# An attention and FFN kernel whose selected weights come from one-hot products instead of gathers

## Chip, cores and metric

One core of a Trainium2 chip. The metric is the device time of one execution in microseconds, lower is better. Engines are TensorE (PE; PEld its weight loads), VectorE (DVE), ScalarE (ACT), GpSimd (POOL), and SyncE (SP), which only issues transfers here.

## What is computed

x is 32 sequences of 32 positions and 512 features in float32. `itok_B_0_30` picks one 32 x 32 matrix out of 32 for each sequence, `itok_B_0_7` an expert; `perm` permutes the features.

```
w = cond_weights[itok_B_0_30]                 # (32, 32, 32), one matrix per sequence
c = einsum('bct,bcd->bdt', x, w)
q, k, v = c @ wq.T, c @ wk.T, c @ wv.T        # 32 heads of 16
q, k = rope(q), rope(k)
x1 = x + softmax(causal(q k^T / 4)) v @ wo.T
h = x1 @ W.T + 2 * sum_e gates[e] * (x1 @ A[e].T) @ B[e].T   # gates: top 2 of 8, softmax
out = x1 + unpermute(down(gelu(up(permute(h)))))
```

## The kernel before

All is written for the five engines by hand: each engine has its own list of instructions, and every wait is on a semaphore (`d_...` for transfers). The 1024 rows are 8 tiles of 128 rows, four sequences each, worked in G = 4 groups g of two tiles t; a group's data stand as features x 256 rows in four chunks of 128. Large products are made in three passes of float32r values (high by high, high by low, low by high: `mm3`, L593 to L595), so each weight has a high half, a copy on ScalarE (`w_his`, L974), and a low half, a subtraction, on VectorE (`w_los`, L1217) or for wo on GpSimd (`wo_los`, L505).

TensorE's order (L589 on) is cond (the selected matrices, spread into `wbd` blocks), q, k, v, scores, the products with the probabilities (`pv`), wo, then the router, the low rank and W products (w2) and the FFN. The stages of successive groups are interleaved: while group g has its `pv`, TensorE makes q, k and v of group g+1. PSUM has eight banks in three rings, A (2: cond, q, k, v), S (2: scores, pv, down) and F (4). Work takes the banks of a ring in turn, and a bank is given back when its reader is done. So the second half of k of group 1 takes the bank from which VectorE's rope(1,1) reads, v(1,0) that of rope(1,2), and v(1,1) that of rope(1,3).

rope(g,i), i = 0, 1 for q and 2, 3 for k, runs on two engines. VectorE shuffles the bank into `rot` (L1261) and multiplies by cos (L1263); GpSimd multiplies `rot` by sin (L474) and adds (L478). There is one `rot` from group 1 on, so VectorE's rope(1,i+1) waits until GpSimd has added rope(1,i) (`ve.wait_ge(roped, n - 1)`). For group 0, rope(0,3) is VectorE's alone (L1269, L1273). k is then spread into `kbd` blocks (`k_blocks`, L489 on GpSimd, L1283 on VectorE). The softmax is max and subtraction on VectorE (`max_shift`, L1295, L1297), exp on ScalarE (L1018), sum and reciprocal on VectorE (`sums`, L1303, L1305), the scaling on GpSimd (`norm`, L535), `turn` on VectorE (L1311), and `probs_block` on ScalarE (L974).

The beginning. GpSimd gathers the rows of cond_weights of group 0 (`cond_rows`, L450) with indices that VectorE makes from the ids, then the 32 whole matrices (`cond_seqs`, L457), which SP writes to a scratch `rows` and reads back for groups 1 to 3 as `wg`. SP holds wq's second half, wk and wv back behind those gathers. Four gathers of w2 and B rows by perm (`perm_rows`, L465) follow on GpSimd once wk has landed; TensorE turns them (`prep_w2`, L602, `prep_b`, L610). Three of the gathered quarters lie in `kbd[1]`, so the k blocks of tile 1 wait for the last `prep_w2`. TensorE runs idle products (L825) while it waits for loads.

GpSimd's list for group 0 is then three ropes, four k blocks, a clearing of pbd, norm(0,0), norm(0,1), wo's low halves, rope(1,0), norm(0,2), norm(0,3), rope(1,1) to rope(1,3) and four k blocks of group 1.

Of the kernel before, what the change touches and what calls it, by code (L numbers as in the profile page):

```python
# [42 lines left out]
MASKED = -1.0e30  # L43

# [36 lines left out]
def build(nc, x, xT, who, wcond, wq, wk, wv, wo, w2b, wr, wa, up, down, perm, consts, cols, rows, out):  # L81
    ctx = ExitStack()
    with ctx:
# [12 lines left out]
        cst = sb("cst", [P, CW])  # L96
# [5 lines left out]
        wg = sb("wg", [P, TILES, T])  # L102
# [16 lines left out]
        small = sb("small", [P, 348])  # L119
        idx = sb("idx", [P, TILES], U32)  # L120
        permc = sb("permc", [P, KC], I32)
# [4 lines left out]
        def rows_of(tile):  # L126
# [7 lines left out]
        kbd1 = kbd[:, 1, :, :, :].rearrange("p c b k -> p (c b k)")  # L134
        WB = D + P
        raw_w2b = [xt[:, 1, :, :].rearrange("p c n -> p (c n)")[:, 0:WB]] + [kbd1[:, WB * c:WB * c + WB]
                                                                            for c in range(KC - 1)]
        raw_a = rows_of(x2[:, 0:2, :].rearrange("p a n -> p (a n)"))
        seq_rows = kr[0:B, :, :].rearrange("p c n -> p (c n)")
# [46 lines left out]
        ids = sb("ids", [P, 3, TILES], I32)  # L186
# [4 lines left out]
        ident = con("ident")  # L191

# [9 lines left out]
        def A(g, k):  # L202
            return "A", 8 * g + k

        def S_at(g):
            return 8 * g - 2 if g else 0

        def S_scores(g, i):
            if g == G - 1:
                return ("A", 8 * G + i) if i < 2 else ("S", S_at(g) + i - 2)  # L210
            return "S", S_at(g) + i

        def PVi(g, t):
            if g == G - 1:
                return "A", 8 * G + 2 + t
            return "S", S_at(g) + 4 + (2 if g else 1) * t
# [12 lines left out]

        f_fill(("w2", 0), ("w2", 1), ("w2", 2), ("b", 0), ("w2", 3))  # L230
# [20 lines left out]
        def Wi(g, i):  # L251
            return ("A", 8 * G + 6) if (g, i) == (G - 1, 1) else Fi(g, "W", i)

        def WOi(g, i):
            return ("A", 8 * G + 4 + i) if g == G - 1 else Fi(g, "WO", i)

        def UNi(i):
            return Fi(G - 1, "UN", 1) if i else ("A", 8 * G + 8)

        def Y_chunk(c):  # L260
            return ("A", 8 * G + 7) if c == KC - 1 else S_down(G - 1, c // 2)
# [15 lines left out]
        def wait_kbd(eng, g, t, c):  # L277

            s = (kbd_v, kbd_p)[c % 2] if g else (kbd_p, kbd_v)[c // 2]
            eng.wait_ge(s, 4 * g + 2 * t + (c // 2 if g else c % 2) + 1)  # L280
# [6 lines left out]
        def half_of(part, r):  # L287

            return xc[:, part, :, :].rearrange("p c (t r n) -> p c t r n", t=GT, r=2)[:, :, :, r, :]

        def by_half(item):
            return bank(item)[:, :].rearrange("p (c t n) -> p c t n", c=KC, t=GT)
# [17 lines left out]
        W_AT = {"wq": 0, "wk": 2, "wv": 4, "wo": 6, "a": 8}  # L310
# [52 lines left out]
        kbd_v, kbd_p, scored = sem("kbd_v"), sem("kbd_p"), sem("scored")  # L363
# [18 lines left out]
        def _(sp):  # L382
# [1239 lines left out]
```

## Time and profile before

| | us |
|---|---|
| median of 3 runs | 217.81 (217.02 to 218.19) |
| the profiled execution | 216.94 |
| its span | 215.1 |
| TensorE busy | 201.6 (94%) |
| VectorE busy | 147.3 (68%) |
| GpSimd busy | 122.4 (57%) |
| ScalarE busy | 114.2 (53%) |

The span is from the first to the last recorded instruction of one execution; the time of an execution is measured around it and is 1.84 us longer here. A timeline row gives start, duration, engine, line, and in brackets how long the engine had been idle and who ended that. A product in float32 is recorded as two rows.

### The profile page before, as it was taken

What the parts mean: (1) busy time and instruction counts of PE and PEld (TensorE: products, weight loads), DVE (VectorE), ACT (ScalarE), POOL (GpSimd) and SP (SyncE); (2) the same over time, 40 slices, a digit from 0 to 9 for tenths busy, and PEclk for the clock granted to TensorE, in tenths of its full rate; (3) what the DMA queues carried; (4) which work ended last, traced back from release to release, by engine and by line L of the source; (5) the groups of instructions that cost most, each with busy time, mean ns of one, the idle gap of its engine ahead of it and who ended that gap; (6) DMA issues with size and microseconds to landing.
All of it is one profiled execution on the core that took longest, in us unless ns stands there. A gap on an engine that the chain in (4) does not pass through costs nothing.

```text
span 215.1 us, 5966 instructions
## 1 busy us (share of the span) xinstructions
PE 201.6 (94%) x2536; PEld 175.2 (81%) x2536; DVE 147.3 (68%) x283; ACT 114.2 (53%) x189; POOL 122.4 (57%) x96
## 2 busy tenths in 40 slices
PE   4999698699999999999999999999999999798993
PEld 4989675598878999988679899986788987688863
DVE  2368799899488978775646877836769886158223
ACT  2173173692271536439983337289865866533460
POOL 6628996959786201487985201978997344425000
PEclk9999999999999999999999999999999999999999
DMA  6699983300001050000026320000044300134002
GB/s 202 194 375 292 337 282 101 91 11 3 0 3 53 0 186 12 5 0 5 0 27 76 101 97 0 3 0 3 0 52 94 56 5 3 10 38 52 0 3 98
DMA packets 10858, 15.43 MB, mean 72 GB/s; under 512 B 2288, under 2 KB 6544, under 8 KB 10832
## 3 DMA queue, kind: packets, MB, share of 16 engines
q1 hardware_dynamic: 8384, 11.99, 16.8%
q0 software_dynamic: 2160, 3.05, 8.7%
q8 instruction: 20, 0.33, 0.6%
q10 hardware_dynamic: 288, 0.01, 0.1%
q14 instruction: 6, 0.05, 0.1%
HBM read 11.25 MB, written 3.80 MB: 70 GB/s over the span
## 4 chain that ended last, share of the span: by engine, by line
PE 86%; DVE 7%; issue 3%; ACT 2%; DMA 1%
PE ps_A L593 12%; PE ps_A L595 11%; PE ps_A L594 11%; PE ps_F L593 8%; PE ps_F L594 7%; PE ps_F L595 7%; PE ps_S L699 6%; PE ps_F L789 4%; PE ps_A L625 4%; PE ps_S L804 3%; PE ps_S L825 3%; PE ps_S L677 3%; PE ps_A L699 1%; PE ps_A L817 1%; DMA cst<-constants 1%
## 5 line engine op out<-in xcount | busy, mean ns | idle before, releaser
L974 ACT ACTIVATE pbd<-pr 32x512 f32<-32x512 f32 x56 | 35.3, 630 | 5.9 <-DVE pr L1311 5.2
L535 POOL TENSOR_TENSOR pr<-pr,small 128x512 f32<-128x512 f32 x16 | 17.6, 1111 | 35.5 <-DVE small L1305 35.4
L474 POOL TENSOR_TENSOR rot<-rot,cst 128x512 f32<-128x512 f32 x14 | 19.1, 1361 | 15.0 <-DVE rot L1261 14.8
L515 POOL DMA_INDIRECT out<-y,row_at x12 | 19.8, 1646 | 11.3 <-ACT y L974 8.8
L1062 ACT ACTIVATE act<-ps_F 128x512 f32<-128x512 f32 x32 | 16.5, 603 | 11.2 <-PE ps_F L789 11.2
L1283 DVE TENSOR_TENSOR kbd<-kr,cst 128x512 f32<-128x512 f32 x16 | 20.7, 1320 | 2.4 <-POOL kr L478 2.4
L489 POOL TENSOR_TENSOR kbd<-kr,cst 128x512 f32<-128x512 f32 x16 | 20.1, 1283 | 2.1 <-PE ps_F L602 2.0
L593 PE MATMUL ps_A<-xc,wqT 128*128 128x256 f32 x64 | 18.2, 285 | 1.7 <-DVE xc L1229 1.7
L1018 ACT ACTIVATE pr<-pr 128x512 f32<-128x512 f32 x16 | 10.0, 631 | 16.4 <-DVE pr L1297 16.2
L593 PE MATMUL ps_A<-xc,wkT 128*128 128x256 f32 x64 | 18.3, 286 | 0.0
L594 PE MATMUL ps_A<-xc,wkT 128*128 128x256 f32 x64 | 17.9, 279 | 0.0
L594 PE MATMUL ps_A<-xc,wqT 128*128 128x256 f32 x64 | 17.9, 279 | 0.0
L595 PE MATMUL ps_A<-xc,wqT 128*128 128x256 f32 x64 | 17.9, 279 | 0.0
L595 PE MATMUL ps_A<-xc,wkT 128*128 128x256 f32 x64 | 17.8, 279 | 0.0
L593 PE MATMUL ps_F<-x,w2T 128*128 128x256 f32 x56 | 16.1, 287 | 0.0
L595 PE MATMUL ps_F<-x,w2T 128*128 128x256 f32 x56 | 15.6, 279 | 0.0
L594 PE MATMUL ps_F<-x,w2T 128*128 128x256 f32 x56 | 15.6, 279 | 0.0
L593 PEld LDWEIGHTS ps_A<-xc,wqT 128*128 128x128 f32 x64 | 12.0, 188 | 2.1 <-issue 1.4
L593 PE MATMUL ps_F<-xc,woT 128*128 128x256 f32 x48 | 13.7, 286 | 0.0
L593 PE MATMUL ps_A<-wvT,xc 128*128 128x512 f32 x32 | 13.5, 420 | 0.0
L594 PE MATMUL ps_F<-xc,woT 128*128 128x256 f32 x48 | 13.4, 280 | 0.0
L595 PE MATMUL ps_F<-xc,woT 128*128 128x256 f32 x48 | 13.4, 279 | 0.0
(187 smaller groups left out, 614.7 us busy)
## 6 DMA issues: line engine op xcount, KB each, us to landing
xs<-in_x SPq DMA_DIRECT2D x4, 512.0 KB, 6.3
xt<-in_xT SPq DMA_DIRECT2D x4, 512.0 KB, 3.3
out<-xt SPq DMA_DIRECT2D x3, 512.0 KB, 3.0
pbd<-in_L_attn_wq SPq DMA_DIRECT2D x2, 512.0 KB, 4.4
act<-in_L_attn_wk SPq DMA_DIRECT2D x1, 1024.0 KB, 6.2
act<-in_L_attn_wv SPq DMA_DIRECT2D x1, 1024.0 KB, 8.6
act<-in_L_attn_wo SPq DMA_DIRECT2D x1, 1024.0 KB, 10.0
out<-xt SPq DMA_DIRECT2D x2, 256.0 KB, 2.2
```

Source lines behind the costliest of these rows:

```text
L474: pool.tensor_tensor(rv, rv, con("sin").unsqueeze(1).to_broadcast([P, 2 * N // T, T]), ALU.mult).then_inc(rot_sin, 1)
L489: pool.tensor_tensor(kbd[:, t, c, :, :].rearrange("p b (h s) -> p b h s", h=HG), kv.unsqueeze(2).to_broadcast([P, BT, HG, T]), con("head") ...
L515: pool.indirect_dma_start(out=out, out_offset=bass.IndirectOffsetOnAxis(ap=row_at[:, g, c:c + 1], axis=0), in_=y[:, c, :], in_offset=None, ...
L535: pool.tensor_tensor(pr[:, i, :, :], pr[:, i, :, :], mx[:, i, :].unsqueeze(2).to_broadcast([P, NH // 2, T]), ALU.mult).then_inc(normed, 1)
L593: pe.matmul(dst, hi_l, hi_r, start=start, stop=False, skip_group_check=skip)
L594: pe.matmul(dst, hi_l, lo_r, start=False, stop=False, skip_group_check=skip)
L595: return pe.matmul(dst, lo_l, hi_r, start=False, stop=stop, skip_group_check=skip)
L699: last = pe.matmul(bank(it)[32 * j:32 * j + 32, P * c:P * c + P], vz_of(g, t)[:, 4 * c + j, HD * e:HD * e + 2 * HD], pbd_of(g, t, c // 2)[ ...
L974: return sc.activation(dst, src, ACT.Copy)
L1018: sc.activation(pr[:, i, :, :], pr[:, i, :, :], ACT.Exp, scale=float(HD) ** -0.5).then_inc(exped, 1)
L1062: sc.activation(act[:, r, j, :, :], bank(it)[:, :].rearrange("p (h n) -> p h n", h=2), ACT.Gelu).then_inc(s_free(it), 1)
L1283: ve.tensor_tensor(kbd[:, t, c, :, :].rearrange("p b (h s) -> p b h s", h=HG), kv.unsqueeze(2).to_broadcast([P, BT, HG, T]), con("head").u ...
```

## The change

The constants bring cond_weights along, laid out so that its 32 matrices lie on partitions. VectorE compares the ids with the partition number (a one-hot), 16 small products (`select`) pick the matrices, four transposes on VectorE put them into `wsel` for all groups, and the `wbd` blocks are made from `wsel`. The three gathers of cond_weights, `rows` and `wg` are gone. x of group 0 is loaded from ScalarE's queue, wq in three pieces, and SP issues wq, wk, wv and x1 with no wait between. GpSimd's `perm_rows` waits for wk as before, and now directly follows two clearings. The gathered rows lie in both halves of `xt`, in `y` and in the third buffer of `vz`, which is therefore cleared after the last `prep_w2`.

cond of group 0 goes to four banks, two chunks each; the q products of group 0 (`first_q`) take both halves chunk by chunk; q and k of group 0 lie in ring F. TensorE makes both v before the first scores, turns w2's quarters 0 and 1 after them, quarter 2 and B after cond(1), and quarter 3 after q of group 1. ScalarE takes three of the k blocks of tile (0,1).

```diff
@@ SP
-            load_x(0)
-            sp.dma_start(raw["wq"][:, 0:2, :], wq_rows[:, 0:2, :]).then_inc(d_w["wq"], 16)
-            sp.wait_ge(d_wg[0], 16)
+            sp.dma_start(raw["wq"][:, 0:1, :], wq_rows[:, 0:1, :]).then_inc(d_w["wq"], 16)
+            sp.dma_start(raw["wq"][:, 1:2, :], wq_rows[:, 1:2, :]).then_inc(d_wq1, 16)
             sp.dma_start(raw["wq"][:, 2:4, :], wq_rows[:, 2:4, :]).then_inc(d_wq2, 16)
-            sp.wait_ge(d_wg[1], 16)
             load_w("wk")
             load_w("wv")
-            sp.wait_ge(d_seq, 16)
-            sp.dma_start(rows, seq_rows).then_inc(d_rows, 16)
             load_x(1)
-            sp.wait_ge(d_rows, 16)
-            sp.dma_start(wg[:, GT:TILES, :],
...
@@ GpSimd
-            pool.wait_ge(idx_ready, 1)
-            cond_rows(0)
-            cond_rows(1)
+            pool.memset(pbd[:, 1, 0:HC, :, :], 0.0).then_inc(pbd_zero, 1)
             pool.wait_ge(d_ids, 16)
-            cond_seqs()
-            pool.memset(pbd[:, 1, :, :, :], 0.0).then_inc(pbd_zero, 1)
-            pool.wait_ge(d_permc, 16)
             pool.wait_ge(d_w["wk"], 16)
             perm_rows()
             for i in range(3):
                 rope(0, i)
-            for t in range(GT):
-                for c in range(2):
-                    k_blocks(0, t, c)
-            wait_w(pool, "wq")
+            k_blocks(0, 0, 0)
+            k_blocks(0, 0, 1)
+            k_blocks(0, 1, 0)
+            wait_w(pool, "wq", KC)
             pool.memset(pbd[:, 0, :, :, :], 0.0).then_inc(pbd_zero, 1)
+            pool.memset(pbd[:, 1, HC:2 * HC, :, :], 0.0).then_inc(pbd_zero, 1)
             for g in range(G):
                 more = g + 1 < G
                 if more:
                     norm(g, 0)
                     norm(g, 1)
                 if g == 0:
+                    wait_full(pool, prep("w2", KC - 1))
+                    pool.memset(vz[:, 2, :, :], 0.0).then_inc(vz_zero, 1)
                     wo_los()
@@ TensorE
+            def select(r):
+
+                it = Fi("sel", r)
+                rows = slice(T * r, T * r + T)
+                for j in range(BT):
+                    at = slice(T * j, T * j + T)
+                    last = pe.matmul(bank(it)[at, 0:SC * T], onehot[rows, at], wst[rows, :],
+                                     start=True, stop=True, skip_group_check=True)
+                last.then_inc(s_full(it), 1)
...
             pe.wait_ge(d_cst, 16)
-            idle_products(16)
-            cond(0, 0)
-            cond(0, 1)
-            idle_products(6)
-            qk(0, "wq", Q, 0)
-            qk(0, "wq", Q, 1)
-            qk(0, "wk", K_, 0)
-            qk(0, "wk", K_, 1)
+            idle_products(2, rings["S"][0])
+            pe.wait_ge(onehot_ready, 1)
+            for r in range(BT):
+                select(r)
+            idle_products(4, rings["S"][0])
+            first_conds()
+            idle_products(2, rings["F"][3])
+            first_q()
+            qk(0, "wk", 0)
+            qk(0, "wk", 1)
+            v(0, 0)
+            v(0, 1)
+            scores(0, 0)
             pe.wait_ge(d_w["w2b"], 16 * KC)
-            for k in range(KC - 1):
-                prep_w2(k)
-            prep_b()
-            wait_w(pe, "wv")
-            v(0, 0)
-            scores(0, 0)
-            prep_w2(KC - 1)
-            v(0, 1)
+            prep_w2(0)
+            prep_w2(1)
             cond(1, 0)
             cond(1, 1)
+            prep_w2(2)
+            prep_b()
             scores(0, 1)
...
                 if g == 0:
+                    prep_w2(KC - 1)
                     pv(0, 0, 0)
@@ ScalarE
             v_out(0, 0)
-            turned_hi(prep("w2", KC - 1), WT["w2"][:, 0, KC - 1, :])
+            for c in range(1, KC):
+                k_blocks(c)
+            v_out(0, 1)
+            turned_hi(prep("w2", 0), WT["w2"][:, 0, 0, :])
             exp(0, 0)
@@ VectorE
+            def turn_selected(r):
+
+                it = Fi("sel", r)
+                wait_full(ve, it)
+                ve.transpose(wsel[:, SC * r:SC * r + SC, :].rearrange("p d t -> p (d t)"),
+                             bank(it)[:, 0:SC * T]).then_inc(s_free(it), 1)
...
-            ve.tensor_scalar(idx[:, :], ids[:, 0, :], float(T), con("pos"), ALU.mult, ALU.add).then_inc(idx_ready, 1)
+            ve.tensor_scalar(onehot, ids[:, 0:BT * T], con("pos"), None, ALU.is_equal).then_inc(onehot_ready, 1)
...
-                    w2_los(2)
                     max_shift(0, 2)
+                    rope(1, 0)
                     max_shift(0, 3)
-                    split_lo(prep("b"), bT[:, 0, :], bT[:, 1, :], prep_hi, KC)
-                    rope(1, 0)
+                    rope(1, 1)
                     sums(0, 2)
                     sums(0, 3)
-                    w2_los(3)
-                    rope(1, 1)
+                    w2_los(1)
                     turn(g, 2)
                     turn(g, 3)
+                    w2_los(2)
                     rope(1, 2)
+                    split_lo(prep("b"), bT[:, 0, :], bT[:, 1, :], prep_hi, KC)
+                    w2_los(3)
                     blocks(2)
                     rope(1, 3)
```

Three places show how the instructions move. First TensorE's beginning, up to q of group 0. Before:

```order
L825 MATMUL ps_S<-cst 128x128 x16
L625 MATMUL ps_A<-wbd,xs 128x64 x16
L825 MATMUL ps_S<-cst 128x128 x6
L593 MATMUL ps_A<-xc,wqT 128x256
```

In the change:

```order
L876 MATMUL ps_S<-cst 128x128 x2
L622 MATMUL ps_F<-cst,y 32x256 x16
L876 MATMUL ps_S<-cst 128x128 x4
L636 MATMUL ps_A<-wbd,xs 128x64 x8
L636 MATMUL ps_S<-wbd,xs 128x64 x8
L876 MATMUL ps_F<-cst 128x128 x2
```

The 16 products of L622 are new, 22 idle products became 8, and cond lies in two rings, chunks 0 and 1 first.

Second GpSimd, from the k blocks of group 0 to rope(1,1). Before:

```order
L489 TENSOR_TENSOR kbd<-kr,cst 128x512 x4
L554 MEMSET pbd 128x2048
L535 TENSOR_TENSOR pr<-pr,small 128x512 x2
L505 TENSOR_TENSOR woT<-act,woT 128x1024 x2
L474 TENSOR_TENSOR rot<-rot,cst 128x512
L478 TENSOR_TENSOR qr<-qr,rot 128x512
L535 TENSOR_TENSOR pr<-pr,small 128x512 x2
```

In the change:

```order
L494 TENSOR_TENSOR kbd<-kr,cst 128x512 x3
L554 MEMSET pbd 128x2048
L555 MEMSET pbd 128x1024
L540 TENSOR_TENSOR pr<-pr,small 128x512 x2
L563 MEMSET vz 128x768
L510 TENSOR_TENSOR woT<-act,woT 128x1024 x2
L481 TENSOR_TENSOR rot<-rot,cst 128x512
L485 TENSOR_TENSOR qr<-qr,rot 128x512
L540 TENSOR_TENSOR pr<-pr,small 128x512 x2
```

The clearing of vz (L563) is new ahead of wo's low halves; it waits until TensorE has turned w2's last quarter.

Third VectorE, rope(1,0) to rope(1,1) and the sums of scores (0,2) and (0,3). Before:

```order
L1261 STREAM_SHUFFLE rot<-ps_A 128x512
L1263 TENSOR_TENSOR qr<-ps_A,cst 128x512
L1303 TENSOR_REDUCE small<-pr 128x16
L1305 RECIPROCAL small<-small 128x16
L1303 TENSOR_REDUCE small<-pr 128x16
L1305 RECIPROCAL small<-small 128x16
L1210 TENSOR_TENSOR w2T<-ps_F,w2T 128x512
L1261 STREAM_SHUFFLE rot<-ps_A 128x512
```

In the change:

```order
L1343 STREAM_SHUFFLE rot<-ps_A 128x512
L1345 TENSOR_TENSOR qr<-ps_A,cst 128x512
L1375 TENSOR_REDUCE small<-ps_S 128x16
L1377 TENSOR_TENSOR pr<-ps_S,small 128x512
L1343 STREAM_SHUFFLE rot<-ps_A 128x512
L1345 TENSOR_TENSOR qr<-ps_A,cst 128x512
L1383 TENSOR_REDUCE small<-pr 128x16
L1385 RECIPROCAL small<-small 128x16
```

The second shuffle, that of rope(1,1), now stands ahead of the sums.

## Rows read from the trace of the kernel before

**Rows 1.** The page, parts 1 and 2: busy sums, 40 slices of 5.4 us.
```profile
PE 201.6 (94%) x2536; PEld 175.2 (81%) x2536; DVE 147.3 (68%) x283; ACT 114.2 (53%) x189; POOL 122.4 (57%) x96
...
PEclk9999999999999999999999999999999999999999
...
GB/s 202 194 375 292 337 282 101 91 11 3 0 3 53 0 186 12 5 0 5 0 27 76 101 97 0 3 0 3 0 52 94 56 5 3 10 38 52 0 3 98
```

**Rows 2.** Busy time by stretch: us, PE, PEld, DVE, ACT, POOL, clock, DMA.
```profile
0.00:13.50 13.50, 9.82 (x76) 9.45 (x77) 4.84 (x18) 4.35 (x5) 7.03 (x9) 1.00 0.72 232
13.50:42.85 29.35, 24.88 (x304) 21.56 (x305) 26.14 (x37) 13.76 (x22) 24.44 (x18) 1.00 0.71 234
...
100.00:150.00 50.00, 50.00 (x659) 43.12 (x662) 33.94 (x63) 31.12 (x53) 29.89 (x23) 1.00 0.17 34
```

**Rows 3.** Timeline of TensorE: start us, us, engine, line, operation, [idle before].
```profile
13.51 0.36 PE L593 MATMUL ps_A<-xc,wqT 128*128 128x256 f32 x1 [0.48 <-DVE xc L1229]
...
24.78 0.28 PE L595 MATMUL ps_A<-xc,wkT 128*128 128x256 f32 x1
...
27.15 0.33 PE L602 MATMUL ps_F<-cst,xt 128*128 128x128 f32 x1 [2.09 <-DMA kbd<-in_w2b,permc]
...
28.87 0.48 PE L593 MATMUL ps_A<-wvT,xc 128*128 128x512 f32 x1
...
31.51 0.40 PE L595 MATMUL ps_A<-wvT,xc 128*128 128x512 f32 x1
...
32.85 1.00 PE L677 MATMUL ps_S<-kbd,qr 64*32 64x128 f32 x48 [0.24 <-POOL kbd L489]
...
38.23 2.00 PE L625 MATMUL ps_A<-wbd,xs 64*128 64x64 f32 x32 [0.78 <-ACT vz L974]
...
40.49 1.16 PE L677 MATMUL ps_S<-kbd,qr 64*32 64x128 f32 x64
...
42.85 0.36 PE L593 MATMUL ps_A<-xc,wqT 128*128 128x256 f32 x1 [1.21 <-DVE xc L1229]
```

**Rows 4.** Timeline of TensorE's weight loads, at v(1,0).
```profile
56.75 0.19 PEld L593 LDWEIGHTS ps_A<-wvT,xc 128*128 128x128 f32 x1 [0.23 <-DVE kr L1263]
```

**Rows 5.** Timeline of GpSimd: the start, and 40 to 54 us.
```profile
0.74 2.02 POOL L447 MEMSET vz<- 128x2304 f32 x1 [0.29 <-POOLq L1603]
...
40.97 4.73 POOL L505 TENSOR_TENSOR woT<-act,woT 128x1024 fp32r<-128x1024 f32 x2
47.94 1.29 POOL L474 TENSOR_TENSOR rot<-rot,cst 128x512 f32<-128x512 f32 x1 [2.24 <-DVE rot L1261]
49.31 1.29 POOL L478 TENSOR_TENSOR qr<-qr,rot 128x512 f32<-128x512 f32 x1
50.56 2.06 POOL L535 TENSOR_TENSOR pr<-pr,small 128x512 f32<-128x512 f32 x2
52.58 1.30 POOL L474 TENSOR_TENSOR rot<-rot,cst 128x512 f32<-128x512 f32 x1
```

**Rows 6.** Timeline of VectorE: setup, k blocks, a transpose, sums.
```profile
4.25 0.46 DVE L1441 CAST ident_b<-cst 32x128 bf16<-32x128 f32 x2
...
30.48 2.86 DVE L1283 TENSOR_TENSOR kbd<-kr,cst 128x512 f32<-128x512 f32 x2
...
41.47 0.70 DVE L1311 STREAM_TRANSPOSE pr<-pr 128x512 f32<-128x512 f32 x1
...
48.35 0.67 DVE L1303 TENSOR_REDUCE small<-pr 128x16 f32<-128x512 f32 x1
...
49.88 0.25 DVE L1305 RECIPROCAL small<-small 128x16 f32<-128x16 f32 x1
```

**Rows 7.** L825 (idle products) alone by stretch: us, PE, PEld, clock, DMA.
```profile
3.20:5.00 1.80, 1.80 (x8) 1.80 (x9) 1.00 1.04 336
...
7.00:8.00 1.00, 1.00 (x6) 1.00 (x6) 1.00 0.38 59
8.00:9.00 1.00, 1.00 (x9) 1.00 (x8) 1.00 0.78 256
```

More of the change, by code:

```diff
@@ L43 @@
 MASKED = -1.0e30
+SC = T // BT
 _AT = {}
@@ L78, in constants, with build @@
     return c
-def build(nc, x, xT, who, wcond, wq, wk, wv, wo, w2b, wr, wa, up, down, perm, consts, cols, rows, out):
+def build(nc, x, xT, who, wq, wk, wv, wo, w2b, wr, wa, up, down, consts, cols, out):
     ctx = ExitStack()
@@ L228, in f_fill @@
                 F_AT[name] = len(F_AT)
+        f_fill(*(("sel", r) for r in range(BT)), ("Q", 0), ("Q", 1), ("K", 0), ("K", 1))
         f_fill(("w2", 0), ("w2", 1), ("w2", 2), ("b", 0), ("w2", 3))
@@ L611, in prep_b, with first_conds @@
                 last.then_inc(s_full(it), 1)
+            def select(r):
[6 more added lines that the diff above has]
+                last.then_inc(s_full(it), 1)
+            def first_conds():
+                pe.wait_ge(d_x[0], 16)
+                pe.wait_ge(wbd_ready, 1)
+                for c in range(KC):
+                    for t in range(GT):
+                        for r in range(2):
+                            it = first_cond(c // 2, r)
+                            rows = slice(P // 2 * r, P // 2 * r + P // 2)
+                            at = P * (c % 2) + P // 2 * t
+                            last = pe.matmul(bank(it)[:, at:at + P // 2], xs[rows, 0, t, P * c:P * c + P],
+                                             wbd[rows, t, :, :], start=True, stop=True, skip_group_check=True)
+                            if t == GT - 1 and c % 2:
+                                last.then_inc(s_full(it), 1)
             def cond(g, t):
                 pe.wait_ge(d_x[g], 16)
-                pe.wait_ge(wbd_ready, g + 2 if g else t + 1)
+                pe.wait_ge(wbd_ready, g + 1)
                 its = [A(g, COND + r) for r in range(2)]
@@ L628, in cond, with first_q, qk @@
                             last.then_inc(s_full(it), 1)
-            def qk(g, name, first, i):
+            def first_q():
+                its = [QK(0, i) for i in range(2)]
+                for it in its:
+                    wait_free(pe, it)
+                W = WT["wq"]
+                for k in range(KC):
+                    wait_w(pe, "wq", k + 1)
+                    if k % 2 == 0:
+                        for r in range(2):
+                            wait_read(pe, first_cond(k // 2, r))
+                    for i, it in enumerate(its):
+                        for h in range(2):
+                            c = 2 * i + h
+                            last = mm3(bank(it)[:, N * h:N * h + N],
+                                       W[:, 0, k, P * c:P * c + P], W[:, 1, k, P * c:P * c + P],
+                                       xc[:, 0, k, :], xc[:, 1, k, :], h == 0 and k == 0, h == 1 and k == KC - 1,
+                                       skip=True)
+                        if k == KC - 1:
+                            last.then_inc(s_full(it), 1)
+            def qk(g, name, i):
                 W = WT[name]
@@ L635, in qk @@
                         wait_read(pe, A(g, COND + r))
-                it = A(g, first + i)
+                it = QK(g, (2 if name == "wk" else 0) + i)
                 wait_free(pe, it)
@@ L1442, in _ @@
                                ).then_inc(mask_ready, 1)
-            ve.wait_ge(d_permc, 16)
+            for r in range(BT):
+                turn_selected(r)
+            blocks(0)
             step(ve.tensor_copy(permf, permc[:, :]))
```

249 lines of the change are left out of this document (134 added, 115 removed).

## Prediction

> **What bounds the kernel now.** I read the page first: TensorE (PE) is busy 94% of a span of 215.1 us [rows 1]. The busy time by stretch [rows 2] says where the rest lies: from 100 to 150 us TensorE is busy all of the 50 us, but in 0 to 13.5 it runs mostly idle products, and from 13.5 to 42.85 it works 24.88 of 29.35 us. So TensorE's own work bounds the kernel from the second tile group on, and a change to the beginning is worth what it moves the point at which TensorE stops waiting. The timeline of TensorE [rows 3] gives the marks: first product of q for group 0 at 13.51, last one of k at 24.78, a wait of 2.09 for the gathered w2 rows ahead of 27.15, and the first q product of group 1 at 42.85 after 1.21 of waiting.
>
> From 42.85 on TensorE looks full, yet it does not run freely. The weight load of v(1,0) at 56.75 was released by VectorE's `kr` of L1263 after 0.23 of waiting [rows 4]: v takes the bank that rope(1,2) reads, and rope(1,2) on VectorE waits until GpSimd has added rope(1,1). GpSimd's rows [rows 5] are a chain: wo's low halves 40.97 to 45.70, rope(1,0) 47.94 to 50.60, the two norms from 50.56, rope(1,1) from 52.58 and so, at the same 2.66, to 55.24, and 1.5 us later v(1,0) starts. **This chain and TensorE arrive together in the kernel before.** Whether the change gains is decided here, not in the beginning that it rewrites.
>
> **The change, part by part.**
>
> Start. The two row gathers, the sequence gather and its trip through memory go; the one-hot goes in. SP's queue loses four waits and two transfers and asks for wq, wk, wv and x1 in one go; x0 moves to ScalarE's queue, behind the ids. The constants' columns grow from 311 to 567 and the ids' from 24 to 140, by 186 KB for 128 partitions, and VectorE waits for both. At 300 GB/s, within the 202 to 375 of the page's first slices [rows 1], that is 0.6 (0.3 if these bytes go first, 1.2 if the x load shares the way equally). VectorE's setup ended at 4.25 + 0.46 = 4.71 [rows 6]; with 0.1 for the longer first instruction it ends at 5.45. The 16 selecting products are small; their nearest rows are the scores, 1.16 for 32 products [rows 3], 36 ns each, up to an idle product's 0.33 at the slow rate [rows 7]: 0.6 to 5.3 us, taken as 1.5, nearest the scores, which also split the array both ways. Four transposes of 256 columns at half of 0.70 [rows 6] and the two block products (taken as 0.8; the strided reading could double that) bring VectorE to 7.8, the index rows to 8.3, wq's two low quarters, 512 columns each and at 0.65 like the sum of 48.35, to 9.6. The first cond products run from 7.9; all took 2.00 [rows 3], so the half that is now waited for takes 1.0, or 2.0 at worst at the slow rate; from cond's end at 40.17 to the next q product were 2.68 us for ScalarE's and VectorE's passes, now over half the columns: 1.5. First q product: between 10.4 and 11.5, **taken as 10.9, which is 2.6 earlier** than 13.51.
>
> Rate at the start. The page gives the granted clock as full, 2.4 GHz, in all slices [rows 1], but an idle product (two rows) takes 0.33 us from 7 to 8 and 0.22 from 8 to 9 [rows 7]. The array is slow for its first 4.8 us, from 3.2 to 8. The new start has gaps between its products, so the slow time may last longer; that is the upper end above. In the same trace a gap of 2.09 us does not bring the slow rate back: four sets of transposes follow in 1.72 us [rows 3].
>
> First group. Both q banks now fill together, 5.65 us after the first product; GpSimd's first rope then starts 6.5 us after it, against 6.2 before, when the gathers held it. The rope and k-block chain had its last block at 30.48 + 2.86 = 33.34 [rows 6], 19.8 us after the first q product, and keeps its links, so the first scores end 20.1 after the new start: 31.0, against about 33.85. TensorE has done both v by then, and w2's gathers, asked for about 3 us sooner since wk lands sooner, are no longer waited for: the 2.09 is gone. Then: two preparations of w2 0.86 (1.72 for four [rows 3]), 0.25 for ScalarE, which now makes three k blocks before it empties the second v bank, cond and scores 3.42 (38.23 to 41.65), two more preparations 0.86. That makes **36.4 for the first q product of group 1, 6.4 earlier than 42.85**. By TensorE's row alone the change gains 6 us.
>
> Where it is lost. GpSimd may not touch wo until the last quarter of w2 has been turned, since it clears the third v buffer, in which the last gathered rows lie, ahead of wo. This quarter is turned only after the 48 q products of group 1, 5.65 us, and its own 0.45: at 42.6. In the kernel before nothing held wo's halves here and they started at 40.97. Then on GpSimd: 0.1 for the semaphore, the clearing 0.67 (a third of 2.02, [rows 5]), wo 4.73, rope(1,0) 2.66: **it ends at 50.8, where it ended at 50.60 before**. The 6 us are gone on this queue. A second step follows. VectorE now does rope(1,1) before the sums of the scores' second pair; rope(1,1) waits for GpSimd's rope(1,0). Before, the sums stood ahead of it, 48.35 to 50.13 [rows 6], and the norms could start at 50.56. Now: rope(1,1) on VectorE 1.4 (the 1.5 less a semaphore), one sum and its reciprocal 0.95, so the norms start at 53.3; two norms 2.02, rope(1,1) on GpSimd 2.67, and the 1.5 to v(1,0): 59.5 against 56.75. **TensorE is 2.7 us later** at v(1,0), after idling some 4.7 us before the second half of k and 4 before v. No wait stands between 56.75 and the first scores of group 1 in the old trace, and GpSimd's k blocks there (two by 67.7, wanted at 69.5) are covered, so all 2.7 pass on to the part where TensorE is full [rows 2].
>
> The three k blocks on ScalarE and the moved loads I cost at nothing beyond the 0.25: ScalarE works 13.76 of the 29.35 us of the stretch [rows 2], and x1, wo and a are asked for earlier than before. If ScalarE were late, cond(1) would move by the same amount and the chain with it.
>
> Sum: the profiled execution took 216.94 for its span of 215.1. 216.94 + 2.7 = 219.6. That execution is 0.87 under the median of 217.81, and what is timed is a median: 217.81 + 2.7 = **220.5**. Bounds of the sum: 42.6 is 40.7 if TensorE never waits (29.8 us of work behind 10.9: q and k of group 0 11.4, two v of 2.87, two scores of 1.48, five preparations of 0.43, cond 1.94, q of group 1 5.65 [rows 3]) and 44 if the start is at 11.5 and the first scores are late, so the shift is +0.8 to +4.1.
>
> **A rule against the rows.** After the two stalls the old trace has no row; its longest gap inside the work is 2.09 us, without harm. The Trainium skill (TensorE: Matmul & The Clock Gate, "Why this matters for your kernels") says that idle gaps between bursts bring the array back to half clock, longer ones than this trace shows. By that rule the stalls of 4.7 and 4 us would have a price; the row of 2.09 us neither bears it out nor excludes it.
>
> **The rivals.**
> (B) As forecast, and the array falls to the slow rate, 1.2 GHz, in the second stall. The first 4.8 us at 0.33 instead of 0.22 for a product lost a third, 1.6 us [rows 7]: that is the price of one such fall. After the first stall it is hidden, since v(1,0) waits for GpSimd anyway; after the second it falls on v. 217.81 + 2.7 + 1.6 = 222.1. For it: gaps double the longest one of before. Against: after the first stall 24 products run, which leaves the second gap shorter.
> (C) The chain is as late as before. If TensorE never waits and the start is at 10.4, w2's last quarter is done by 40.2, and the shift is about +0.3: 218.1. For it: VectorE's long operations beside GpSimd (2.86 for two blocks) may shorten when the order shifts.
> (D) Faster. The chain in GpSimd only counts from the turned quarter at 39.9 on; if that comes earlier, each us is gained. It takes a first q product at 9 and a scores chain of 18 us in place of 20.1, which puts the quarter at 38.5 and the time at 216.4. For it: VectorE's contended rows (blocks, adds) leave 2 us. Against: VectorE's row alone reaches 9.55 before it may touch cond.
> (E) That the change does little of what its name says: GpSimd's w2 gathers waited for wk before as well, so this wait is no change; only wk lands sooner. It is no case of its own.
>
> **How the numbers follow.** A change under 0.5%, 1.1 us, can't be told from none. Forecast (shift +1.1 to +3.7): 0.52, its own range 218.9 to 221.5. B: 0.18. C: 0.16. D: 0.14. Slower is 0.52 + 0.18 = 0.70, same 0.16, faster 0.14. The range 217.3 to 222.9 leaves out most of D and the upper part of B.
>
> **What would show it.** In the new trace: first q product of group 0 at 10.4 to 11.5; first q product of group 1 near 36.4; wo's halves on GpSimd right behind the last turned w2 quarter near 42.6; rope(1,0) on GpSimd ending near 50.8; TensorE idle about 4.7 us before the second half of k of group 1, released by VectorE; norms starting near 53.3; v(1,0) near 59.5. Wrong would be: wo's halves started before 40, no idle of over 1 us on TensorE between 37 and 60, or weight loads twice as long behind a stall (then B).

## The result and the profile after

| | before | after |
|---|---|---|
| median of 4 runs each, us | 217.71 (217.02 to 218.19) | 220.40 (220.18 to 222.41) |
| ratio, 95% interval | | 1.0146 [1.0081, 1.0212] |
| profiled execution, us (span) | 216.94 (215.1) | 220.18 (218.4) |
| mean granted clock | 1.0 | 0.984 |

Repeated with six runs of the changed kernel, the ratio was 1.0143 [1.0102, 1.0183]. The change makes the kernel about 1.4% slower, 2.7 us in the medians. Here and below a median is over all runs and a ratio leaves out the executions in a slower state, so the ratio can differ a little from the quotient of the medians. The page of the changed kernel, parts 1 and 2, beside [rows 1]:

```profile
PE 200.8 (92%) x2540; PEld 173.3 (79%) x2540; DVE 147.4 (67%) x287; ACT 118.1 (54%) x205; POOL 119.6 (55%) x94
...
PEclk9999999997599999999999999999999999999999
```

TensorE's busy time is 0.8 less and the span 3.3 longer, and the tenth and eleventh of the 40 slices show a clock that was not at full speed. TensorE's timeline of the changed kernel says where the time went (start us, us, engine, line, operation, idle before and what ended it); it answers to [rows 3, 4]:

```profile
8.48 1.11 PE L636 MATMUL ps_A<-wbd,xs 64*128 64x64 f32 x16 [0.28 <-DVE wbd L1330]
...
10.91 0.36 PE L596 MATMUL ps_F<-xc,wqT 128*128 128x256 f32 x1
...
24.95 0.50 PE L596 MATMUL ps_A<-wvT,xc 128*128 128x512 f32 x1 [1.20 <-DVE wvT L1292]
...
30.84 1.00 PE L728 MATMUL ps_S<-kbd,qr 64*32 64x128 f32 x48 [0.72 <-POOL kbd L494]
...
37.16 0.38 PE L596 MATMUL ps_A<-xc,wqT 128*128 128x256 f32 x1
...
42.91 0.38 PE L605 MATMUL ps_F<-cst,xt 128*128 128x128 f32 x2
...
53.04 0.58 PE L596 MATMUL ps_A<-xc,wkT 128*128 128x256 f32 x1 [4.51 <-DVE qr L1345]
...
60.09 0.50 PE L596 MATMUL ps_A<-wvT,xc 128*128 128x512 f32 x1 [1.55 <-DVE kr L1345]
```

The new beginning does its part: the first q product comes at 10.91 instead of 13.51, and group 1's at 37.16 instead of 42.85, 5.7 us sooner. Then TensorE waits 4.51 us before the second half of k and again before v(1,0), which starts at 60.09 instead of 56.75. The 5.7 us become a loss of 3.3 within 23 us. GpSimd's timeline over the same stretch, against [rows 5]:

```profile
43.58 0.74 POOL L563 MEMSET vz<- 128x768 f32 x1 [3.81 <-PE ps_F L605]
44.27 4.72 POOL L510 TENSOR_TENSOR woT<-act,woT 128x1024 fp32r<-128x1024 f32 x2
48.95 1.26 POOL L481 TENSOR_TENSOR rot<-rot,cst 128x512 f32<-128x512 f32 x1
50.30 1.26 POOL L485 TENSOR_TENSOR qr<-qr,rot 128x512 f32<-128x512 f32 x1
53.95 2.06 POOL L540 TENSOR_TENSOR pr<-pr,small 128x512 f32<-128x512 f32 x2 [2.39 <-DVE small L1385]
55.96 1.28 POOL L481 TENSOR_TENSOR rot<-rot,cst 128x512 f32<-128x512 f32 x1
```

It stands idle 3.81 us until TensorE has turned the last quarter of w2, then does the clearing, wo's halves and rope(1,0), which ends at 51.56 (50.60 before); then it waits 2.39 for the sums that now stand behind rope(1,1) on VectorE. The norms start 3.4 us later than before, and v(1,0) is 3.3 later. Busy time by stretch (us, PE, PEld, DVE, ACT, POOL, granted clock, DMA) shows what the waiting did to the clock:

```profile
48.00:53.00 5.00, 0.53 (x20) 0.26 (x12) 1.32 (x4) 0.00 (x0) 3.48 (x3) 0.93 0.27 102
53.00:58.00 5.00, 4.96 (x23) 4.96 (x24) 4.08 (x8) 2.07 (x4) 3.98 (x4) 0.50 0.00 0
58.00:60.00 2.00, 0.53 (x3) 0.24 (x2) 1.28 (x4) 0.44 (x1) 1.06 (x2) 0.71 0.00 0
60.00:62.00 2.00, 1.91 (x8) 1.61 (x9) 2.00 (x4) 0.00 (x0) 1.92 (x2) 1.00 0.00 0
```

Behind the wait of 4.51 the second half of k ran at 1.2 GHz and took 5.5 us (53.04 to 58.54), where it takes 3.1 at full clock (49.22 to 52.30 in the repeated run of both edits below). That costs nothing, since v(1,0) waits for VectorE anyway; it only shortens the second wait, to 1.55. The clock was back at full speed when v started (1.00 from 60 on). The Trainium skill (TensorE: Matmul & The Clock Gate, "Why this matters for your kernels") has long idle gaps between bursts bring the half clock back, and this trace agrees: 0.50 behind 4.51 us.

### The profile page after: what moved, and what is told of

It reads as the page before. It is cut to its first block, busy times and chain, and to the rows that moved or that the text cites. A ratio compares the mean times of both kernels' runs of the same rounds, so it can differ in the third digit from the quotient of the medians.

```text
span 218.4 us, 6001 instructions
## 1 busy us (share of the span) xinstructions
PE 200.8 (92%) x2540; PEld 173.3 (79%) x2540; DVE 147.4 (67%) x287; ACT 118.1 (54%) x205; POOL 119.6 (55%) x94
## 4 chain that ended last, share of the span: by engine, by line
PE 70%; POOL 14%; issue 5%; DMA 4%; DVE 4%; ACT 1%; SPq 1%; DVEq 0%; POOLq 0%
PE ps_A L596 8%; PE ps_F L596 8%; PE ps_A L598 7%; PE ps_A L597 7%; PE ps_F L597 7%; PE ps_F L598 7%; PE ps_S L750 5%; PE ps_F L840 4%; DMA act<-in_L_attn_wk 4%; PE ps_S L728 3%; PE ps_S L855 3%; POOL rot L481 3%; PE ps_A L653 3%; POOL woT L510 2%; POOL qr L485 2%
## 5 line engine op out<-in xcount | busy, mean ns | idle before, releaser
L540 POOL TENSOR_TENSOR pr<-pr,small 128x512 f32<-128x512 f32 x16 | 17.6, 1110 | 40.2 <-DVE small L1385 40.1
L1363 DVE TENSOR_TENSOR kbd<-kr,cst 128x512 f32<-128x512 f32 x14 | 19.3, 1408 | 2.4 <-POOL kr L485 2.4
L494 POOL TENSOR_TENSOR kbd<-kr,cst 128x512 f32<-128x512 f32 x15 | 19.5, 1330 | 0.1
L596 PE MATMUL ps_A<-xc,wkT 128*128 128x256 f32 x48 | 15.0, 312 | 4.5 <-DVE qr L1345 4.5
L597 PE MATMUL ps_A<-xc,wkT 128*128 128x256 f32 x48 | 14.5, 302 | 0.0
L598 PE MATMUL ps_A<-xc,wkT 128*128 128x256 f32 x48 | 14.5, 301 | 0.0
L596 PEld LDWEIGHTS ps_A<-xc,wkT 128*128 128x128 f32 x48 | 10.1, 211 | 5.4 <-DVE qr L1345 4.8
L596 PE MATMUL ps_A<-xc,wqT 128*128 128x256 f32 x48 | 13.7, 285 | 0.0
L597 PE MATMUL ps_A<-xc,wqT 128*128 128x256 f32 x48 | 13.4, 280 | 0.0
L598 PE MATMUL ps_A<-xc,wqT 128*128 128x256 f32 x48 | 13.4, 280 | 0.0
```

What stands on the lines that cost most here:

```text
L494: pool.tensor_tensor(kbd[:, t, c, :, :].rearrange("p b (h s) -> p b h s", h=HG), kv.unsqueeze(2).to_broadcast([P, BT, HG, T]), con("head") ...
L540: pool.tensor_tensor(pr[:, i, :, :], pr[:, i, :, :], mx[:, i, :].unsqueeze(2).to_broadcast([P, NH // 2, T]), ALU.mult).then_inc(normed, 1)
L596: pe.matmul(dst, hi_l, hi_r, start=start, stop=False, skip_group_check=skip)
L597: pe.matmul(dst, hi_l, lo_r, start=False, stop=False, skip_group_check=skip)
L598: return pe.matmul(dst, lo_l, hi_r, start=False, stop=stop, skip_group_check=skip)
L1363: ve.tensor_tensor(kbd[:, t, c, :, :].rearrange("p b (h s) -> p b h s", h=HG), kv.unsqueeze(2).to_broadcast([P, BT, HG, T]), con("head").u ...
```

## The experiments

My theory: the beginning gains some 6 us, and two orders on the helper engines take it back. These are (1) GpSimd's wait for w2's last quarter ahead of wo's halves and rope(1,0), and (2) rope(1,1) ahead of the sums on VectorE. The rivals: the half clock costs the time itself, or the gathers of w2, held back for wk, do. Medians with the ratio against the kernel before on the same chip:

| run | us | ratio, 95% |
|---|---|---|
| sums first (e1_sums_first) | 219.73 | 1.0044 [0.9995, 1.0093] |
| wo free (e2_wo_free) | 219.25 | 1.0006 [0.9950, 1.0062] |
| both (e3_both) | 215.05 | 0.9847 [0.9765, 0.9928] |
| swap in the kernel before (e4_before_swap) | 222.31 | 1.0193 [1.0137, 1.0250] |
| first wait filled (e5_warm) | 226.09 | 1.0269 [1.0201, 1.0337] |
| gathers early (e6_gather_early) | 226.76 | 1.0333 [1.0277, 1.0389] |
| both, wv sooner (e7_both_wv) | 218.38 | 0.9913 [0.9873, 0.9952] |
| wo free, filled (e8_wo_free_warm) | 219.08 | 0.9954 [0.9917, 0.9991] |
| after again (f1_after) | 221.24 | 1.0143 [1.0102, 1.0183] |
| both again (f2_both) | 215.90 | 0.9900 [0.9857, 0.9942] |
| both, early products (f3_both_zeros) | 214.19 | 0.9829 [0.9798, 0.9860] |
| both waits filled (f4_warm_both) | 221.68 | 1.0163 [1.0113, 1.0212] |

The first four shared one chip (before: 218.26), the next four another (219.90), the last four a third (218.32). The kernel before differs by 0.7% between these chips, so ratios are compared, not times. Two more things help in reading the profiles. In every profile without a half clock behind v(1,0), what follows v(1,0) takes the same time on a chip: 159.8 us on the second chip, and 158.2 to 158.4 on the other two and in the profiles of before and after above. And the start of the changed kernel and its variants comes in two kinds, with the first q product near 10.9 or near 12.9 (shown at the end of this part); the profiles of e1, e2 and f2 are of the early kind, those of e3, e5, e7, e8, f1 and f4 of the late one, and f3 and e6 are told below.

### The two orders, one at a time and together

**Sums first.** VectorE's list for group 0 in the changed kernel:

```diff
-                    rope(1, 1)
                     sums(0, 2)
                     sums(0, 3)
+                    rope(1, 1)
```

> The changed kernel with VectorE's sums of scores (0,2) and (0,3) put back ahead of rope(1,1). Theory (GpSimd's chain decides): the norms can start when GpSimd ends rope(1,0), at 51.6 instead of 53.95; rope(1,1) and all behind it come 2.3 us sooner, v(1,0) at 57.8 instead of 60.1, unless the k half in front, which still runs at the low clock behind the 4.5 us stall, ends at 58.2 and sets it: gain 1.8 to 2.3, so 218.1 to 218.6. Rival (the clock's fall or the new beginning costs the time): the stall and its clock stay, so no gain, 220.4.

From 1.0146 to 1.0044 is 1.0%, 2.2 us, though the two intervals still overlap; the profiles are the stronger evidence. GpSimd's timeline of this run:

```profile
50.34 1.26 POOL L485 TENSOR_TENSOR qr<-qr,rot 128x512 f32<-128x512 f32 x1
51.55 2.05 POOL L540 TENSOR_TENSOR pr<-pr,small 128x512 f32<-128x512 f32 x2
53.56 1.28 POOL L481 TENSOR_TENSOR rot<-rot,cst 128x512 f32<-128x512 f32 x1
```

The norms follow rope(1,0) at once, 2.4 us sooner, v(1,0) starts at 57.71 in place of 60.09, and the profiled span is 2.4 shorter (216.0). The k half still runs slowly at its start (53.08 to 57.6), and now ends as v becomes ready. In the profiles the step is worth what the chain said.

**Wo free.** On GpSimd, the wait and the clearing move behind rope(1,0):

```diff
                 if g == 0:
-                    wait_full(pool, prep("w2", KC - 1))
-                    pool.memset(vz[:, 2, :, :], 0.0).then_inc(vz_zero, 1)
                     wo_los()
...
                     rope(g + 1, 0)
+                if g == 0:
+                    wait_full(pool, prep("w2", KC - 1))
+                    pool.memset(vz[:, 2, :, :], 0.0).then_inc(vz_zero, 1)
```

> The changed kernel with the wait for w2's last quarter and the clearing of vz moved behind rope(1,0) on GpSimd, so that wo's low halves need not wait. Theory: wo's halves start at 39.8 instead of 44.3, rope(1,0) ends at 47.1 instead of 51.6, and with the sums still behind rope(1,1) v(1,0) starts near 55.8: gain 4.3, so 216.1; the stall before the second k half shrinks from 4.5 to under 1 and the clock stays at 1.00. Rival (GpSimd's place is hidden, TensorE waits for something else): no gain.

The order did what it should and the time did not: v(1,0) is 3.8 us sooner than in the changed kernel, the profiled span only 0.9 shorter (217.5). TensorE's row and the stretches say why:

```profile
56.28 0.80 PE L597 MATMUL ps_A<-wvT,xc 128*128 128x512 f32 x1 [3.94 <-DVE kr L1346]
```
```profile
56.00:58.00 2.00, 1.72 (x4) 1.43 (x5) 2.00 (x4) 0.00 (x0) 1.92 (x2) 0.50 0.00 0
58.00:62.00 4.00, 4.00 (x17) 2.66 (x20) 1.84 (x5) 0.13 (x1) 2.93 (x4) 0.50 0.00 0
```

The wait before k is gone, k runs at full clock and ends sooner, and the whole wait, 3.94, now stands before v(1,0). The clock falls there, on products that something waits for: 6 us at half clock cost 2.9 (from v(1,0) to the end this profile takes 161.2 us, the one before it 158.3), and 3.8 less 2.9 is the 0.9 that is left. The forecast of 216.1 missed this: it had the clock at 1.00.

**Both edits** in one kernel:

> Both edits together. Theory: rope(1,0) ends at 47.1, the norms run from 47.9 (behind the clearing), v(1,0) starts near 54.1, 6 us sooner than in the changed kernel and 2.6 sooner than in the kernel before: 214.4. Then the new beginning's gain shows at last. Rival (the two edits mend the same wait): no better than the second alone, 216.1.

It measured 0.9847, then 0.9900 on another chip beside the unaltered changed kernel (1.0143); both gave their medians within 1 us of each other.

> The changed kernel again, unaltered, as the partner of the three that follow on the same chip. Forecast: 1.2 to 1.5% over the kernel before if the products of the start run at the full clock from 8.5 on; where the first cond half takes 1.97 us instead of 1.11, as in the runs of the last four experiments, the first q product is near 12 instead of 10.9 and all behind it about 2 us later, so 1.0 to 2.5%.

> The third experiment's kernel again (wo's halves not held back, sums ahead of rope(1,1)). Theory: 6 us under the unaltered changed kernel on the same chip (v(1,0) six us sooner, no stall over 2 us before it). Rival (its 215.05 was a lucky state of the start): 2 to 3 us under it.

On that chip the two orders together are 5.3 us, 221.24 to 215.90. GpSimd's and TensorE's rows of the repeated run:

```profile
39.75 4.74 POOL L510 TENSOR_TENSOR woT<-act,woT 128x1024 fp32r<-128x1024 f32 x2
44.47 1.28 POOL L481 TENSOR_TENSOR rot<-rot,cst 128x512 f32<-128x512 f32 x1
45.83 1.30 POOL L485 TENSOR_TENSOR qr<-qr,rot 128x512 f32<-128x512 f32 x1
47.05 0.75 POOL L567 MEMSET vz<- 128x768 f32 x1
47.75 2.06 POOL L540 TENSOR_TENSOR pr<-pr,small 128x512 f32<-128x512 f32 x2
```
```profile
53.92 0.50 PE L597 MATMUL ps_A<-wvT,xc 128*128 128x512 f32 x1 [1.62 <-DVE kr L1346]
```

The chain on GpSimd no longer has a gap, v(1,0) starts at 53.92, 2.8 before the kernel before, after a wait of 1.62, and the clock stayed at 1.00. So the new beginning does gain, once the queues let it through.

**The swap alone, in the kernel before:** rope(1,1) ahead of the sums and of the w2 halves on VectorE, and nothing else.

> The kernel before with one change only: VectorE's rope(1,1) ahead of the sums of scores (0,2) and (0,3), as in the changed kernel. Theory: rope(1,0) still ends at 50.6, the norms start near 53.0 instead of 50.56, v(1,0) near 59.1 instead of 56.75: 2.4 slower, 220.1. Rival (the order on VectorE is hidden): 217.7.

It cost 4.0 us (1.0193), more than I forecast.

```profile
56.11 2.06 POOL L535 TENSOR_TENSOR pr<-pr,small 128x512 f32<-128x512 f32 x2 [2.41 <-DVE small L1305]
```
```profile
62.25 0.50 PE L593 MATMUL ps_A<-wvT,xc 128*128 128x512 f32 x1 [2.42 <-DVE kr L1263]
```

GpSimd waits 2.41 for the sums, as in the changed kernel (2.39), and TensorE 2.42 before v(1,0), about the 2.4 of the forecast. The rest is clock:

```profile
62.00:64.00 2.00, 1.75 (x5) 1.48 (x6) 1.19 (x3) 0.00 (x0) 1.92 (x2) 0.71 0.00 0
64.00:66.00 2.00, 2.00 (x6) 1.54 (x5) 1.32 (x3) 0.00 (x0) 1.05 (x2) 0.50 0.00 0
```

From v(1,0) to the end it takes 159.8 us where the kernel before takes 158.4 (56.75 to 215.1): 1.4 for the clock. The profiled execution was longer still (span 222.0), since its first q product of group 1 came 3.1 us late, at 45.97: wk landed 1.4 us later (GpSimd's first gather at 16.03 instead of 14.67), and why it did is not settled.

### The clock: is it the price, and where

**First wait filled.** Idle products in the changed kernel, in the wait before the second k half:

```diff
                     pv(0, 0, 3)
+                    wait_free(pe, PVi(0, 1))
+                    idle_products(20, bank(PVi(0, 1)))
                     qk(1, "wk", 1)
```

> The changed kernel with 20 idle products put into TensorE's 4.5 us stall ahead of the second k half of group 1 (into the bank of pv(0,1), once it is free). The granted clock should stay at 1.00, where it fell to 0.50 from 53 to 58, and this k half take 2.8 us instead of 5.2. Theory (GpSimd's chain sets v(1,0), the slow half is hidden in front of it): v(1,0) still starts near 60.1, 220.4, no gain. Rival (the clock costs the time): up to 2.4 us faster, 218.0.

It became slower, 1.0269 against 1.0146, which neither the theory nor the rival had. Its rows:

```profile
62.26 0.80 PE L596 MATMUL ps_A<-wvT,xc 128*128 128x512 f32 x1 [3.95 <-DVE kr L1347]
```
```profile
53.00:58.00 5.00, 5.00 (x45) 4.94 (x44) 4.06 (x9) 0.00 (x0) 2.60 (x3) 1.00 0.00 0
...
62.00:64.00 2.00, 1.74 (x4) 1.45 (x5) 2.00 (x4) 0.00 (x0) 1.92 (x2) 0.50 0.03 8
64.00:68.00 4.00, 4.00 (x17) 2.66 (x20) 1.83 (x5) 0.15 (x1) 2.93 (x4) 0.50 0.00 0
```

k ran at full clock, the whole wait moved to v, and so did the half clock: 6 us of it, where it is not hidden.

**Both waits filled**, with 14 more idle products before v(1,0):

> The changed kernel with idle products in both stalls, 20 ahead of the second k half and 14 ahead of v(1,0). Theory (filling only the first stall moved the clock's fall to the second, where v runs behind it unhidden and cost 2 to 3 us): now nothing runs at the low clock and v(1,0) starts when GpSimd's chain lets it, so the time is that of the unaltered changed kernel, within 0.5 us. Rival (idle products cost time in themselves): 2 to 3 us over it, as with the first stall filled alone.

```profile
62.56 0.50 PE L596 MATMUL ps_A<-wvT,xc 128*128 128x512 f32 x1 [0.84 <-DVE kr L1349]
```

The clock stayed at 1.00 throughout, v(1,0) starts at the same place (62.56, against 62.11 in the profiled execution of the unaltered kernel on this chip), and the time is the same within what can be told: 1.0163 against 1.0143. So the half clock behind the first wait costs the changed kernel nothing that these runs can tell, and the rival falls: the loss is the chain. The price of a fall before v is read on one chip at a time. With the first wait filled, what follows v(1,0) takes 162.4 us; in the three other profiles of that chip it takes 159.8, so the price is 2.6, close to the 2.9 of wo free.

**Wo free, with its one wait filled** (14 idle products before v(1,0)):

> The second experiment's kernel (wo's halves not held back) with 14 idle products in the stall of 3.9 us ahead of v(1,0), where its clock fell to 0.50 until 62.9. Theory (chain plus clock): v(1,0) keeps its start near 56.3 and v, pv and v run at full clock, so the 4.3 us that the chain gave appear: 216.1, about 3 less than the second experiment's 219.25. Rival (the second experiment was slow for another reason): 219.

From 1.0006 to 0.9954 is 0.5%, less than the 2.9 us that wo free lost to the clock; the intervals overlap, so it is a size I can't give, and the forecast of 216.1 was missed. In its profile v(1,0) starts at 57.46 behind 0.81 of idle, at full clock, and what follows takes the 159.8 us of its chip, so the fall is gone. But this profile is of the late kind (first q product at 12.85, 10.83 in that of wo free), and v(1,0) is 1.2 later. In the medians the order stays behind both edits (0.9900, 0.9847), filled or not.

### The beginning

**Gathers early.** The gathers of w2 and B are no longer held back until wk has landed. Both kernels have this hold; the gathers of cond_weights, which the change removes, are not touched:

```diff
             pool.wait_ge(d_ids, 16)
-            pool.wait_ge(d_w["wk"], 16)
             perm_rows()
```

> The changed kernel with GpSimd's four gathers of w2 and B rows not held back until wk has landed; they are asked for at 4.2. Theory: the gathered rows are wanted at 31 and lie there in time either way, and GpSimd is idle from 3 to 11.9; the 1.3 MB now go ahead of wq's last part, wk and wv, which land up to 3.5 us later. wk's low halves are wanted at 16.5 and are done at 15.2, so up to 2.2 us later starts of k of group 0: 220.4 to 222.6, likelier 221.5. Rival (the hold is a cost): faster, since GpSimd's first rope no longer waits behind the gathers (2.3 us): 218.1.

It is 1.9% slower than the changed kernel, about 4 us by the ratios, more than I gave it. VectorE's timeline of this run, and TensorE's:

```profile
6.42 0.45 DVE L1318 STREAM_TRANSPOSE wsel<-ps_F 128x256 f32<-128x256 f32 x1 [0.48 <-issue]
7.35 0.45 DVE L1318 STREAM_TRANSPOSE wsel<-ps_F 128x256 f32<-128x256 f32 x1 [0.48 <-PE ps_F L621]
8.83 0.45 DVE L1318 STREAM_TRANSPOSE wsel<-ps_F 128x256 f32<-128x256 f32 x1 [1.03 <-remote]
10.34 0.45 DVE L1318 STREAM_TRANSPOSE wsel<-ps_F 128x256 f32<-128x256 f32 x1 [1.05 <-remote]
```
```profile
11.53 1.98 PE L635 MATMUL ps_A<-wbd,xs 64*128 64x64 f32 x16 [3.17 <-DVE wbd L1329]
```

In the changed kernel the four transposes are one piece, 6.30 to 7.74. Here GpSimd issues its gathers from 4.53 to 9.48, and the transposes lie 0.5 to 1.05 us apart; TensorE waits 3.17 for them, and its granted clock is 0.50 from 12 to 18. The first cond product is 3.1 us later than in other profiles of the late kind (11.53 against 8.46), and so is the first q product (16.01 against 12.94): all of this is there before wk is needed, so it isn't the loads that I had blamed. At v(1,0) 2.5 are left (64.64 against 62.11). Holding the gathers back pays. That their issue is what delays VectorE is likely by the times and not shown: what exactly holds it ("remote" names no instruction of this core) stays open.

**Both, and wv's second low half ahead of rope(0,2)** on VectorE, to end the wait of 1.20 at 24.95:

> Both edits of the third experiment, and the low half of wv's second part taken before rope(0,2) on VectorE, in its 2.5 us of idle time. Theory: TensorE's wait of 1.2 us in v(0,0) goes and rope(0,3) starts 0.9 sooner, but v(1,0) hangs on GpSimd's chain, which starts from the norms; they move by the 0.9 too: 0.9 under the third experiment, 214.1. Rival (the first group's order is hidden): 215.

A miss: 0.9913, no better than both edits alone (0.9847 and 0.9900). Its rows:

```profile
23.30 2.29 POOL L481 TENSOR_TENSOR x<-x,cst 128x512 f32<-128x512 f32 x1
```
```profile
22.30 2.12 DVE L1293 TENSOR_TENSOR wvT<-act,wvT 128x1024 fp32r<-128x1024 f32 x1
```

Its profile and that of e3_both are both of the late kind, and there TensorE doesn't wait for wv in either, so this start had no such wait to remove. GpSimd's product with sin in rope(0,1) took 2.29 in place of 1.30 beside the moved instruction (in e3_both it is that of rope(0,2) which takes 2.29, beside the same subtraction). VectorE then waited 1.41 for GpSimd ahead of rope(0,3), whose product with sin took 1.81 in place of 0.68, and the first norms came at 40.85 where both edits alone had them at 39.88.

**Both, with six products on a cleared buffer** ahead of the constants' landing:

```diff
+            pe.wait_ge(vz_zero, 1)
+            zeros = vz[:, 0:2, :, :].rearrange("p a b c -> p (a b c)")
+            for _ in range(6):
+                pe.matmul(rings["S"][0][:, 0:P], zeros[:, 0:P], zeros[:, P:2 * P], start=True, stop=True)
             pe.wait_ge(d_cst, 16)
```

> The same, and six products on the zeros of the cleared vz ahead of the constants' arrival, so that TensorE is active from 2.2 instead of 4.0. Theory (the array is slow for its first 4.8 us of activity): the cond products run at the full clock in every execution, the first q product is at 10.9 or sooner, and the spread goes: 2 us under the kernel without them where that one starts slowly. Rival (products of zeros do not count, or the late full clock has another cause): no difference.

The six runs of both edits lay in two groups, near 214.1 and near 216 (214.03 to 216.41); with the early products all six are within 213.59 to 214.57. The profiles show the two kinds: in some executions of these kernels the first cond half takes 1.11 and q starts near 10.9, in others this:

```profile
8.46 1.97 PE L636 MATMUL ps_A<-wbd,xs 64*128 64x64 f32 x16 [0.18 <-DVE wbd L1330]
10.19 1.95 PE L636 MATMUL ps_S<-wbd,xs 64*128 64x64 f32 x16
12.94 0.56 PE L596 MATMUL ps_F<-xc,wqT 128*128 128x256 f32 x1
```

That is the unaltered changed kernel again, 2.0 us later at q than in its first profile. In the kernel with early products, TensorE's rows read

```profile
2.17 2.93 PE L882 MATMUL ps_S<-vz 128*128 128x128 f32 x12 [2.17 <-POOL vz L468]
...
9.21 1.11 PE L637 MATMUL ps_A<-wbd,xs 64*128 64x64 f32 x16 [0.92 <-DVE wbd L1335]
```

TensorE starts at 2.17 instead of 4.00, and cond takes the short 1.11. Not all went as expected: the first q product is at 11.63, later than the 10.92 of an early start, since the selecting products now start 0.7 later. So the gain, 1.7 us in the medians (the intervals just touch), is that of fewer late starts. Why there are two kinds is open. The theory's form, slow for the first 4.8 us of activity, doesn't hold: in f1_after TensorE is active from 3.96 and its products stand 0.21 apart up to 16.3. At 214.19 it is the fastest version here, 1.7% under the kernel before and 7.1 us under the changed one. No run here puts such early products into the kernel before, whose runs spread as widely (216.90 to 219.66 on this chip).

## Why the prediction was right

The measured 220.40 stands beside a forecast of 220.5, a shift of +2.7 beside +2.7. The mechanism held; that the numbers agree to 0.1 is partly luck, since the executions of one kernel differ by 2 us and the points below are off by up to 0.9. Point by point:

- **Start.** First q product forecast at 10.9, measured 10.91. The cond half took 1.11 for the 1.0 taken; the other bound, 2.0 at the slow rate, is what other executions of the same kernel show (1.97); their first q product, at 12.94, lies outside my 10.4 to 11.5.
- **First group.** First q product of group 1 forecast at 36.4, measured 37.16. The gathers' 2.09 went as said; two waits came that I had not: 1.20 for wv's low half, and 0.72 for `kbd`, so the scores ended at 31.84 and not at 31.0. Both hang on GpSimd, which still issued gathers until 18.41 and began its first rope at 18.54, 7.6 us after the first q product where I had 6.5:

```profile
18.54 1.29 POOL L481 TENSOR_TENSOR rot<-rot,cst 128x512 f32<-128x512 f32 x1
```
```profile
21.30 0.01 DVE L1343 LOAD_MASK_SELECT rot<-ps_F  x1 [2.52 <-POOL qr L485]
22.57 2.33 DVE L1292 TENSOR_TENSOR wvT<-act,wvT 128x1024 fp32r<-128x1024 f32 x1
```

  VectorE had made `rot` ready at 16.99, waited 2.52 for GpSimd's add, and came to wv's second low half only at 22.57, which v now wants directly behind k. I had costed that step at nothing.
- **Where it is lost.** The main step held. Wo's halves were to start behind the last turned quarter and a clearing, at 43.4; they did at 44.27, since the quarter came 0.9 later with the rest. Rope(1,0) ended at 51.56 (50.8 forecast), norms at 53.95 (53.3), v(1,0) at 60.09 (59.5). Each is 0.6 to 0.9 late and the differences between them are right to about 0.1. (The working has a slip of 0.1: 36.4, 5.65 and 0.45 make 42.5, not 42.6.) Both edits together undo exactly this and turn 1.0143 into 0.9900.
- **The second wait** was mis-sized: 4 us forecast, 1.55 measured. The clock fell behind the first wait, and k took 2.4 longer. Had k run at full clock, the wait would be 4.0, which the run with the first wait filled shows (3.95).
- **The sum.** The profiled execution shifted by +3.2 (216.94 to 220.18), the medians by +2.7. The 0.6 at v(1,0) that I was short of is seen in the one and not in the other.
- **Rival B** had its mechanism right and its place wrong: I had the fall behind the second wait, at 1.6 us. It came behind the first, hidden, as that rival's own sentence allowed. The sign I had set for it, weight loads twice as long behind a stall, was therefore nearly met (0.33 us each in place of 0.19) without B being true: a sign has to name the place too. Its price was too small: where v was hit, it was 2.9 (wo free) and 2.6 (first wait filled). I had taken it from idle products, which lose a third at the slow rate (0.33 against 0.22), where the q and k products lose nearly half (0.21 apart against 0.12).
- **Rivals C and D** needed TensorE not to wait in group 0, or the quarter turned by 40.2 and 38.5; it was turned from 42.91. **E** stands: in the changed kernel the gathers are issued at 11.91 to 17.45, and the hold on wk is no change. But that hold is not idle: without it the changed kernel is 1.9% slower.

## What to carry to other kernels

A gain at the start is worth what reaches the point where all engines meet. Follow each helper engine's queue to that point, and look for a wait for early work that stands in front of work that is due, since it takes back the gain at once and the page's busy shares don't show it. When two waits of TensorE follow each other, look at both before mending one: removing or filling the first alone moved the half clock from a place where it was hidden to one where it was not. Filling both only kept the time; mending both gained.

## What the runs showed of the hardware

- The granted clock fell behind waits of 4.51, 3.95, 3.94 and 3.17 us (the last at the start of e6_gather_early) and, in the swapped kernel before, 2.42; behind 1.62 and 1.64 (both edits) and 2.09 (the kernel before) it did not. Behind the 2.42 it fell only when TensorE had already worked again for half a us: 1.00 up to 62.75, 0.50 from 63. Which length decides is not settled by these.
- At the start the page gives the clock as full, yet the same 16 products take 1.11 or 1.97 us and q products stand 0.21 or 0.12 apart, from one execution to the next. The granted clock in the records can't be trusted there (in f1_after until 16.3); the products' own times can. With six products started at 2.17 the profiled execution had the short time, and all six times lay within 1.0 us.
- In the run in which GpSimd issued gathers from 4.53 to 9.48, VectorE's transposes of that time stood 0.48 to 1.05 us apart, where they otherwise stand in one piece.
- A product or an add of 128x512 on GpSimd takes 1.3 us, also beside VectorE's shuffles, and 2.16 to 2.36 in some places of the ropes of group 0. In the profiles before, after, e3_both and e7_both_wv each such place lies beside VectorE's subtraction for wv's low half, and moves with it. So moving a VectorE instruction changes the length of its neighbours.
